# One-core cross-attention and ternary FFN: turning the second batch's operands by DMA, third scores moved forward, w2 loaded by GpSimd's queue

## The chip, the cores and the metric

One NeuronCore of a Trainium2 chip runs the whole kernel. The metric is the device time of one execution in microseconds (us). A core has TensorE (PE, matmul; PEld is its weight load), VectorE (DVE), ScalarE (ACT), GpSimd (POOL) and SyncE (SP), which here only issues DMAs. Each engine works through its own instructions in the order in which they are written, and stops where a semaphore has not reached the value waited for.

## The reference, cut to what matters

For each of B = 4 batches (512 rows of 512):

```
query, key = ctx @ Wq.T + bq, ctx @ Wk.T + bk     # ctx 512x256, Wq/Wk 128x256
probs      = softmax(query @ key.T)               # 512x512
x          = x + layernorm(x) @ probs
w1q, w2q   = ternary(w1), ternary(w2)             # clip(round(w / mean|w|), -1, 1)
h          = gelu(layernorm(x) @ w1q.T + b1)      # 2048 wide
out        = x + h @ w2q.T + b2
```

The scale of a ternary matrix is the mean over all of its 1M elements, so no weight can be rounded before the whole matrix has arrived and its absolute values are summed.

## The kernel before, in words

The program is written out engine by engine; nothing is scheduled automatically. `B1, W1, W2` number three sums over all partitions. Matmul operands of the attention and of the hidden layer are fp32 values split in two fp16 parts, "hi" (a cast on ACT) and "lo" (a subtraction on DVE), and must lie transposed in SBUF.

- `xn` (normalised x) and `probs` of a batch are written by POOL. For batches 0 and 1 (`b < EARLY`) PE transposes them in fp32 into PSUM (`turn_xn`, `turn_probs`, 16 transposes each, L454 and L467), ACT casts PSUM to the hi part (L661, L656) and DVE makes the lo part (L776, L770). For batches 2 and 3 ACT and DVE write hi and lo into a staging area in SBUF (L684, L689; L793, L799), and SP transposes each of the four by DMA (L258).
- `project` (L435) makes query and key, `scores` (L443) the score matrix, `attend` (L494) the attention: 12 matmuls for each of 4 row tiles. `maximum` (DVE, L804) and `exps` (ACT, L650) follow the scores; `residual` (DVE, L829) adds the attention to x; `moments2` (L835) and `aggregate2` make the statistics from which POOL (`layernorm2`, L373) writes `x2n`.
- `high_x2` (ACT, L674) and `low_x2` (DVE, L784) stage `x2n`, `turn_x2` and, for batch 0 in two halves, `turn_first_x2` (SP, L271) transpose it into `x2T`.
- `sum_abs` (ACT, L698) sums |w| of one of 8 chunks of a weight matrix, `abs_rows` (DVE, L849) adds the chunks, `total` (PE, L473) sums over partitions by a matmul with ones, `quantiser_scale` (DVE, L853) makes the scale. `round_weights` (POOL, L393 and L396) rounds chunk after chunk, `quantise` (DVE, L894) clips it, `turn_w1`, `turn_w2` (SP, L290, L298) transpose it.
- `hidden` (L511) is the first FFN matmul, in four groups of four 128-wide pieces; `first_output` (L525) and `output` (L536) are the second.

The place of the change is the stretch before the first `hidden`. On PE its order is written out by hand:

```
            scores(1, range(NT), lambda t: pe.wait_ge(xn0_read, t + 1))
            turn_xn(1)
            attend(0, lambda t: pe.wait_ge(exp_done, NT + t + 1), [0, 1])
            turn_probs(1)
            attend(0, lambda t: pe.wait_ge(exp_done, NT + t + 1), [2, 3])
            pe.wait_ge(bank_read[3], N_PROBS1 + 1)
            total(W1, ps_t[3])
```

then three tiles of `attend(1)`, `project(2)`, its fourth tile, `total(W2)`, `scores(2)`, and `hidden(0, 0)`. `hidden(0, 0)` waits for all four transposes of `x2T` of batch 0 and for the first piece of w1. The DMA queue of SP is likewise one list: loads of ctx, x, w1, w2, ctx again, b2 and x, and then the transposes.

Of the kernel before, what the change touches and what calls it, by code (L numbers as in the profile page):

```python
# [25 lines left out]
def xattn_ffn(nc, x, ctx_in, Wq, bq, Wk, bk, w1, b1, w2, b2, out):  # L26
# [4 lines left out]
    P = 128  # L31
# [10 lines left out]
    EARLY = 2  # L42
    LAST = B - 1
# [3 lines left out]
    with ExitStack() as stack:  # L47
# [109 lines left out]
        xnT_here = [sem(f"xnT_here{b}") for b in range(EARLY, B)]  # L157
        probsT_here = [sem(f"probsT_here{b}") for b in range(EARLY, B)]

# [82 lines left out]
        def _(sp):  # L242
# [9 lines left out]
            def load_w(m, h):  # L252
                n = raws[m].shape[1] // 4
                for i in (2 * h, 2 * h + 1):
                    sp.dma_start(raws[m][:, i * n:(i + 1) * n, :], w_views[m][:, i * n:(i + 1) * n, :]).then_inc(w_here[m][h], 16)
# [18 lines left out]
            def turn_xn(b):  # L274
                if b > EARLY:
                    sp.wait_ge(attn_ready, NT * b)
                sp.wait_ge(xn_hi_done, NT * (b - EARLY + 1))
                turn(xnT(b), xn_stage(b), 0, xnT_here[b - EARLY])
                sp.wait_ge(xn_lo_done, NT * (b - EARLY + 1))
                turn(xnT(b), xn_stage(b), 1, xnT_here[b - EARLY])  # L280

            def turn_probs(b):
                sp.wait_ge(probs_hi_done, NT * (b - EARLY + 1))
                turn(probsT(b), probs_stage(b), 0, probsT_here[b - EARLY])
                sp.wait_ge(probs_lo_done, NT * (b - EARLY + 1))
                turn(probsT(b), probs_stage(b), 1, probsT_here[b - EARLY])
# [38 lines left out]
            load_ctx(3)  # L325
            for c in range(NCH):
# [18 lines left out]
        def _(pool):  # L345
# [735 lines left out]
```

## Time and profile before

| | |
|---|---|
| median of 3 runs | 312.29 us (311.95 to 313.38) |
| profiled execution | 312.49 us, span of its trace 310.7 us |
| PE busy | 303.9 us, 98% of the span |
| DVE, ACT, POOL busy | 153.7, 143.9, 109.2 us |
| granted TensorE clock | 1.00 |
| first `hidden` matmul starts at | 59.32 us |

The profile counts from the start of the span. "Landing" of a DMA is the time from the start of its issue to its last completion. The chain of waits follows the work that ended last back to the beginning: each piece in it begins where the piece before it ended.

### The profile page before, as it was taken

How to read it: one execution, taken by the hardware profiler on the slowest of the kernel's cores; microseconds unless marked ns; L12 is line 12 of the kernel's file. 1: busy time of each engine (PE TensorE's matmuls, PEld its weight loads, DVE VectorE, ACT ScalarE, POOL GpSimd, SP SyncE). 2: the span in 40 equal slices, each digit the busy share in tenths (PEclk: the TensorE clock that was granted, in tenths of full speed). 3: DMA queues.
4: the chain of work that ended last, by engine and by line, in shares of the span. 5: the costliest groups of instructions: out<-in, count | busy, mean ns of one | idle time of the engine just before them, and what ended most of it. 6: DMA issues, size and time to landing. Idle time of an engine off the chain costs nothing.

```text
span 310.7 us, 3674 instructions
## 1 busy us (share of the span) xinstructions
PE 303.9 (98%) x1401; PEld 144.2 (46%) x1401; DVE 153.7 (49%) x295; ACT 143.9 (46%) x253; POOL 109.2 (35%) x111
## 2 busy tenths in 40 slices
PE   6799999999999999999999999999999999999996
PEld 3366544444444444444444444444444444444455
DVE  0888896764598853755308342445433003442101
ACT  2179998577723506542654604545440017762000
POOL 0276339999979960000903620000650000000000
PEclk9999999999999999999999999999999999999999
DMA  7899999674653992000032854000034100000011
GB/s 174 237 381 408 361 277 205 131 135 103 121 104 63 155 228 105 2 0 0 0 70 54 166 103 154 0 0 0 2 69 115 56 34 0 0 2 0 34 49 54
DMA packets 66706, 32.24 MB, mean 104 GB/s; under 512 B 59504, under 2 KB 60032, under 8 KB 66176
## 3 DMA queue, kind: packets, MB, share of 16 engines
q1 hardware_dynamic: 66368, 31.73, 40.4%
q10 hardware_dynamic: 320, 0.27, 0.4%
q8 instruction: 11, 0.18, 0.2%
q14 instruction: 7, 0.06, 0.1%
HBM read 15.21 MB, written 4.19 MB: 62 GB/s over the span
## 4 chain that ended last, share of the span: by engine, by line
PE 96%; DMA 2%; DVE 1%; SPq 0%; ACT 0%; issue 0%
PE ps_t L511 36%; PE ps_e L536 24%; PE ps_e L494 13%; PE ps_e L525 9%; PE ps_e L443 5%; PE ps_e L435 2%; PE ps_e L543 2%; PE ps_t L435 2%; DMA ctx_sb<-in_ctx 2%; PE ps_t L467 1%; PE ps_e L454 1%; PE ps_t L454 1%; SPq L247 0%; DVE ctxT L764 0%; ACT qkT L644 0%; DVE x_sb L1055 0%
## 5 line engine op out<-in xcount | busy, mean ns | idle before, releaser
L511 PE MATMUL ps_t<-x2T,w1T 128*128 128x512 f16 x512 | 112.1, 379 | 0.0
L706 ACT ACTIVATE ps_t<-ps_t,b_col 128x512 f32<-128x512 f32 x64 | 42.5, 665 | 96.6 <-PE ps_t L511 96.6
L511 PEld LDWEIGHTS ps_t<-x2T,w1T 128*128 128x128 f16 x512 | 50.1, 98 | 60.7 <-issue 0.6
L900 DVE SCALAR_TENSOR_TENSOR gT_lo<-ps_t,h_scale,gT_hi 128x512 f16<-128x512 f32 x64 | 45.1, 746 | 66.2 <-ACT gT_hi L711 66.2
L536 PE MATMUL ps_e<-w_raw,gT_hi 128*128 128x512 f16 x176 | 66.7, 379 | 0.0
L536 PE MATMUL ps_e<-w_raw,gT_lo 128*128 128x512 f16 x176 | 66.7, 379 | 0.0
L349 POOL TENSOR_TENSOR rstd<-var_eps,minus_half 128x4 f32<-128x4 f32 (+1 forms) x9 | 8.5, 947 | 99.7 <-DVE neg_mean L813 99.7
L711 ACT ACTIVATE gT_hi<-ps_t,h_scale 128x512 f16<-128x512 f32 x64 | 40.3, 684 | 0.0
L906 DVE SCALAR_TENSOR_TENSOR x_sb<-ps_e,h_unscale,x_sb 128x512 f32<-128x512 f32 x15 | 11.0, 748 | 57.9 <-PE ps_e L536 54.6
L536 PEld LDWEIGHTS ps_e<-w_raw,gT_lo 128*128 128x128 f16 x176 | 17.2, 98 | 21.4 <-issue 1.0
L536 PEld LDWEIGHTS ps_e<-w_raw,gT_hi 128*128 128x128 f16 x176 | 17.2, 98 | 21.1 <-issue 0.7
L525 PE MATMUL ps_e<-w_raw,gT_hi 128*128 128x512 f16 x64 | 24.3, 379 | 0.0
L525 PE MATMUL ps_e<-w_raw,gT_lo 128*128 128x512 f16 x64 | 24.3, 379 | 0.0
L494 PE MATMUL ps_e<-w_raw 128*128 128x512 f16 x96 | 21.7, 379 | 0.0
L387 POOL TENSOR_TENSOR x_sb<-x_sb,b_sb 128x512 f32<-128x512 f32 x16 | 21.0, 1343 | 0.0
L379 POOL TENSOR_SCALAR probs<-probs,row_inv 128x512 f32<-128x512 f32 x16 | 14.7, 935 | 17.3 <-DVE row_inv L809 17.3
L393 POOL TENSOR_SCALAR w_raw<-w_raw,inv_scale 128x1024 f32<-128x1024 f32 x16 | 20.8, 1301 | 0.0
L650 ACT ACTIVATE probs<-ps_e,row_max 128x512 f32<-128x512 f32 x16 | 10.9, 686 | 15.0 <-DVE row_max L804 14.7
L396 POOL TENSOR_SCALAR w_raw<-w_raw 128x1024 f16<-128x1024 f32 x16 | 17.2, 1074 | 1.4
L698 ACT ACTIVATE abs_out<-w_raw 128x1024 uint8<-128x1024 f32 x16 | 17.1, 1066 | 0.4
L443 PE MATMUL ps_e<-qkT 128*128 128x512 f32 x32 | 14.7, 598 | 0.7 <-ACT qkT L644 0.7
L494 PEld LDWEIGHTS ps_e<-w_raw 128*128 128x128 f16 x96 | 9.4, 98 | 11.3
(86 smaller groups left out, 290.9 us busy)
## 6 DMA issues: line engine op xcount, KB each, us to landing
w_raw<-in_L_ffn_w SPq DMA_DIRECT2D x8, 1024.0 KB, 14.7
x_sb<-in_x SPq DMA_DIRECT2D x4, 1024.0 KB, 7.5
out<-x_sb SPq DMA_DIRECT2D x15, 256.0 KB, 2.6
ctx_sb<-in_ctx SPq DMA_DIRECT2D x16, 128.0 KB, 3.2
b_sb<-in_L_ffn_b SPq DMA_DIRECT2D x1, 256.0 KB, 7.2
w_raw<-w_raw SPq DMA_TRANSPOSE x16, 3.8
out<-x_sb SPq DMA_DIRECT2D x2, 128.0 KB, 1.7
x2n<-in_L_xattn_Wq ACTq DMA_DIRECT2D x1, 128.0 KB, 3.0
```

The costliest lines, as they stand in the source:

```text
L387: nc.gpsimd.tensor_tensor(x_sb[:, b, t], x_sb[:, b, t], b2_sb[:], ALU.add).then_inc(b2_added, 1)
L393: nc.gpsimd.tensor_scalar(src, src, inv_scale[:, m:m + 1], ROUND, ALU.mult, ALU.add).then_inc(scaled, 1)
L396: nc.gpsimd.tensor_scalar(chunk_whole(m, c), src, -ROUND, 1.0, ALU.add, ALU.mult).then_inc(rounded, 1)
L443: nc.tensor.matmul(scores_bank(b, t)[:], qkT[:, 0, t * P:(t + 1) * P], qkT[:, 1], start=True, stop=True).then_inc(scores_ready, 1)
L494: mm = nc.tensor.matmul(attn_bank(b, t)[:], xnT(b)[:, u, j, t * P:(t + 1) * P], probsT(b)[:, v, j], start=(n == 0 and j == 0), stop=(n == ...
L511: mm = nc.tensor.matmul(ps_t[t][:], w1T[:, k, j], x2T[:, b % 2, v, :, j], start=(v == 0 and j == 0), stop=(v == 1 and j == ND - 1))
L525: mm = nc.tensor.matmul(y_bank(0, t)[:], part[:, k, t * P:(t + 1) * P], w2T[:, k], start=(k == 0 and part is gT_hi), stop=(k == NF - 1 and ...
L536: mm = nc.tensor.matmul(y_bank(b, t)[:], part[:, k, t * P:(t + 1) * P], w2T[:, k], start=(k == 0 and part is gT_hi), stop=(k == NF - 1 and ...
L698: nc.scalar.activation(abs_out[:], flat[:, c * CH:(c + 1) * CH], ACT.Abs, accum_out=abs_sum[:, m, c:c + 1]).then_inc(abs_done, 1)
L706: nc.scalar.activation(ps_t[t][:], ps_t[t][:], ACT.Gelu, scale=1.0 / LN_SCALE, bias=b1_col[:, k:k + 1]).then_inc(gelu_done, 1)
L711: nc.scalar.activation(gT_hi[:, k], ps_t[t][:], ACT.Identity, scale=h_scale[:, 0:1]).then_inc(gT_hi_done, 1)
L900: nc.vector.scalar_tensor_tensor(out=gT_lo[:, k], in0=ps_t[t][:], scalar=h_scale[:, 0:1], in1=gT_hi[:, k], op0=ALU.mult, op1=ALU.subtract) ...
```

## The change

Three things. First, batch 1 is handled as batches 2 and 3 are: ACT and DVE write hi and lo of `xn` and `probs` into staging areas (`x2T[:, 1]` and the upper half of `gT_lo`, not yet in use) and SP transposes them into `gT_hi` by DMA, so that PE no longer transposes them. Second, on PE `project(2)`, `total(W1)` and `scores(2)` stand between the whole of `attend(0)` and the whole of `attend(1)`, and `total(W2)` moves behind `hidden(0, 0)`. The lists of ACT and DVE are rewritten to match. Third, w2 is loaded by four DMAs of GpSimd's queue after `normalise_probs(1)`; on SP's queue the loads of b2 and of x of batches 2 and 3 go behind the transposes of w1.

```diff
+    BY_PE = 1
...
         def xn_stage(b):
+            if b < EARLY:
+                return x2T[:, 1].rearrange("p v h j t -> p v (h j t)")
             return w2_stage[:, 0]
...
         def probs_stage(b):
+            if b < EARLY:
+                return lo_stage[:, 1]
             return w2_stage[:, 1]
...
             load_x(1)
-            load_w(0, 0)
-            load_w(0, 1)
-            load_w(1, 0)
-            load_w(1, 1)
+            load_w1(0)
+            load_w1(1)
             load_ctx(2)
-            sp.dma_start(b2_sb[:], b2.rearrange("(a d) -> a d", a=1).to_broadcast([P, D])).then_inc(b2_here, 16)
-            load_x(2)
-            load_x(3)
+            turn_xn(1)
+            turn_probs(1)
             turn_first_x2(0)
             turn_w1(0)
             turn_first_x2(1)
...
             load_ctx(3)
+            sp.dma_start(b2_sb[:], b2.rearrange("(a d) -> a d", a=1).to_broadcast([P, D])).then_inc(b2_here, 16)
+            load_x(2)
+            load_x(3)
...
+            def load_w2():
+                for j in range(ND):
+                    pool.dma_start(w2_raw[:, j], w_views[1][:, j]).then_inc(w_here[1][j // 2], 16)
...
             normalise_probs(1)
+            load_w2()
             layernorm2(0, range(0, 2), 0)
...
-            turn_xn(1)
-            attend(0, lambda t: pe.wait_ge(exp_done, NT + t + 1), [0, 1])
-            turn_probs(1)
-            attend(0, lambda t: pe.wait_ge(exp_done, NT + t + 1), [2, 3])
-            pe.wait_ge(bank_read[3], N_PROBS1 + 1)
+            attend(0, lambda t: pe.wait_ge(exp_done, NT + t + 1), range(NT))
+            project(2, lambda s: pe.wait_ge(bank_read[s], N_PROBS0 + 1))
+            pe.wait_ge(bank_read[3], N_PROBS0 + 1)
             total(W1, ps_t[3])
-            attend(1, lambda t: pe.wait_ge(x2_done, t + 1), range(3))
-            project(2, lambda s: pe.wait_ge(bank_read[s], N_PROBS1 + 1))
-            attend(1, lambda t: pe.wait_ge(x2_done, t + 1), [3])
-            pe.wait_ge(total_read, W1 + 1)
-            total(W2, ps_t[3])
-            scores(2, range(NT), lambda t: pe.wait_ge(x2_done, NT + t + 1))
+            scores(2, range(NT), lambda t: pe.wait_ge(x2_done, t + 1))
+            attend(1, lambda t: pe.wait_ge(exp_done, NT * EARLY + t + 1), range(NT))
...
-            for g in range(GROUPS):
+            hidden(0, 0)
+            pe.wait_ge(x2_done, 2 * NT)
+            total(W2, ps_e[3])
+            for g in range(1, GROUPS):
                 hidden(0, g)
```

ScalarE's order at this place, from the exponentials of batch 1 on. In the rows L650 is `exps`, L661 and L656 the casts of the transposed `xn` and `probs`, L698 `sum_abs`, L674 `high_x2`, L644 the copy of query and key. Before:

```order
L650 ACTIVATE probs,row_sum<-ps_e,row_max 128x512 x4
L661 CAST gT_hi<-ps_t 128x512 x4
L698 ACTIVATE abs_out,abs_sum<-w_raw 128x1024 x4
L656 CAST gT_hi<-ps_t 128x512 x4
L698 ACTIVATE abs_out,abs_sum<-w_raw 128x1024 x2
L674 CAST gT_lo<-x2n 128x4x128 x2
L698 ACTIVATE abs_out,abs_sum<-w_raw 128x1024 x3
L674 CAST gT_lo<-x2n 128x4x128 x2
L698 ACTIVATE abs_out,abs_sum<-w_raw 128x1024 x4
L644 ACTIVATE qkT<-ps_t,bqk 128x512 x2
L698 ACTIVATE abs_out,abs_sum<-w_raw 128x1024
```

And of the change, where each line number is one lower and L683 and L688 write the staging areas:

```order
L649 ACTIVATE probs,row_sum<-ps_e,row_max 128x512 x4
L683 CAST x2T<-xn 128x4x128 x4
L688 CAST gT_lo<-probs 128x4x128 x4
L697 ACTIVATE abs_out,abs_sum<-w_raw 128x1024 x4
L643 ACTIVATE qkT<-ps_t,bqk 128x512 x2
L697 ACTIVATE abs_out,abs_sum<-w_raw 128x1024 x2
L673 CAST gT_lo<-x2n 128x4x128 x2
L649 ACTIVATE probs,row_sum<-ps_e,row_max 128x512 x4
L673 CAST gT_lo<-x2n 128x4x128 x2
L697 ACTIVATE abs_out,abs_sum<-w_raw 128x1024 x8
```

The copy of query and key of batch 2 now stands ahead of the last two absolute sums of w1; all eight of w2 stand behind the third exponentials.

VectorE's order around the first clipped weights. L784 is `low_x2`, L764 `turn_ctx(2)`, L829 `residual`, L894 `quantise`, L853 and L856 `quantiser_scale`. Before:

```order
L853 TENSOR_SCALAR scale<-ps_t 128x1
L856 RECIPROCAL inv_scale<-scale 128x1
L784 TENSOR_TENSOR gT_lo<-x2n,gT_lo 128x4x128 x2
L764 STREAM_TRANSPOSE ctxT<-ctx_sb 128x16x2x32
L829 SCALAR_TENSOR_TENSOR x_sb<-ps_e,x_sb 128x512
L784 TENSOR_TENSOR gT_lo<-x2n,gT_lo 128x4x128 x2
L894 TENSOR_SCALAR w_raw<-w_raw 128x1024
```

And of the change, where L846 is `abs_rows(W1)`, L801 `maximum` of batch 2, L806 `inverse`, and L781, L826 and L891 are `low_x2`, `residual` and `quantise`:

```order
L846 TENSOR_REDUCE abs_row<-abs_sum 128x1
L801 TENSOR_REDUCE row_max<-ps_e 128x1 x2
L850 TENSOR_SCALAR scale<-ps_t 128x1
L853 RECIPROCAL inv_scale<-scale 128x1
L801 TENSOR_REDUCE row_max<-ps_e 128x1 x2
L781 TENSOR_TENSOR gT_lo<-x2n,gT_lo 128x4x128 x4
L806 RECIPROCAL row_inv<-row_sum 128x1 x4
L826 SCALAR_TENSOR_TENSOR x_sb<-ps_e,x_sb 128x512
L891 TENSOR_SCALAR w_raw<-w_raw 128x1024
```

`low_x2` now stands behind the four maxima of batch 2, and the first `quantise` behind all of it.

## Rows read from the trace of the kernel before

**Rows 1.** The page: busy time of each engine.

```profile
PE 303.9 (98%) x1401; PEld 144.2 (46%) x1401; DVE 153.7 (49%) x295; ACT 143.9 (46%) x253; POOL 109.2 (35%) x111
```

**Rows 2.** Chain of waits in order of time: start, us, what.

```profile
27.79 1.75 PE ps_t L454 x16
29.54 5.18 PE ps_e L494 x24
...
41.85 7.79 PE ps_e L494 x36
49.64 3.43 PE ps_t L435 x8
...
55.78 3.54 PE ps_e L443 x8
59.32 27.63 PE ps_t L511 x128
```

**Rows 3.** Timeline of ScalarE: start, us, instruction, idle before and its releaser.

```profile
27.61 0.68 ACT L650 ACTIVATE probs<-ps_e,row_max 128x512 f32<-128x512 f32 x1
...
30.18 0.21 ACT L650 ACTIVATION_READ_ACCUMULATOR probs<-ps_e,row_max 128x1 f32 x1
...
43.25 1.06 ACT L698 ACTIVATE abs_out<-w_raw 128x1024 uint8<-128x1024 f32 x1
...
44.44 1.06 ACT L698 ACTIVATE abs_out<-w_raw 128x1024 uint8<-128x1024 f32 x1
...
174.69 2.16 ACT L689 CAST w_raw<-probs 128x512 f16<-128x512 f32 x4
```

**Rows 4.** Timeline of VectorE.

```profile
43.77 1.27 DVE L784 TENSOR_TENSOR gT_lo<-x2n,gT_lo 128x512 f16<-128x512 f32 x2
44.96 1.24 DVE L764 STREAM_TRANSPOSE ctxT<-ctx_sb 128x1024 f32<-128x1024 f32 x1
...
46.70 2.80 DVE L784 TENSOR_TENSOR gT_lo<-x2n,gT_lo 128x512 f16<-128x512 f32 x2
49.42 0.41 DVE L894 TENSOR_SCALAR w_raw<-w_raw 128x1024 f16<-128x1024 f16 x1
49.76 0.68 DVE L829 SCALAR_TENSOR_TENSOR x_sb<-ps_e,x_sb 128x512 f32<-128x512 f32 x1
...
58.70 1.36 DVE L804 TENSOR_REDUCE row_max<-ps_e 128x1 f32<-128x512 f32 x2
...
60.65 0.41 DVE L809 RECIPROCAL row_inv<-row_sum 128x1 f32<-128x1 f32 x4
```

**Rows 5.** Timeline of GpSimd.

```profile
28.93 2.69 POOL L379 TENSOR_SCALAR probs<-probs,row_inv 128x512 f32<-128x512 f32 x4 [2.55 <-DVE row_inv L809]
...
47.61 1.36 POOL L396 TENSOR_SCALAR w_raw<-w_raw 128x1024 f16<-128x1024 f32 x1
...
50.83 1.04 POOL L396 TENSOR_SCALAR w_raw<-w_raw 128x1024 f16<-128x1024 f32 x1
```

**Rows 6.** Timeline of SP's queue: issue start, us that issuing took.

```profile
49.87 1.45 SPq L290 DMA_TRANSPOSE w1T<-w_raw  x1
51.36 2.69 SPq L271 DMA_TRANSPOSE x2T<-gT_lo  x2
```

**Rows 7.** L271, the transpose issued at 52.7 alone.

```profile
DMA to landing us min/median/max: 3.3/3.3/3.3
```

**Rows 8.** L255, the fourth load of w1 alone, issued at 13.55.

```profile
DMA to landing us min/median/max: 15.5/15.5/15.5
```

**Rows 9.** L255, all loads of w1 and w2; the last has the longest landing.

```profile
L255 SPq DMA_DIRECT2D w_raw<-in_L_ffn_w x8: 507/694/3829, 11.7 to 21.8; - x8
...
DMA to landing us min/median/max: 9.3/14.7/17.8
```

**Rows 10.** L258, transposes of a whole staged half (16 blocks), all eight.

```profile
DMA to landing us min/median/max: 4.3/4.7/5.0
```

**Rows 11.** Timeline of TensorE, its first matmuls.

```profile
1.17 4.21 PE L428 MATMUL ps_e<-gT_lo 128*128 128x512 f16 x10 [1.17 <-DVE gT_lo L910]
```

More of the change, by code:

```diff
@@ L156, in xattn_ffn @@
         x2T_here = [sem(f"x2T_here{b}") for b in range(B)]
-        xnT_here = [sem(f"xnT_here{b}") for b in range(EARLY, B)]
-        probsT_here = [sem(f"probsT_here{b}") for b in range(EARLY, B)]
+        xnT_here = [sem(f"xnT_here{b}") for b in range(BY_PE, B)]
+        probsT_here = [sem(f"probsT_here{b}") for b in range(BY_PE, B)]
         ident_zero, ident_done = sem("ident_zero"), sem("ident_done")
@@ L250, in load_x, with load_w1 @@
                 sp.dma_start(x_sb[:, b], x_tiles[b]).then_inc(x_here[b], 16)
[L252 to L253 removed]
+            def load_w1(h):
+                n = NF // 4
                 for i in (2 * h, 2 * h + 1):
[L255 removed]
+                    sp.dma_start(w1_raw[:, i * n:(i + 1) * n], w_views[0][:, i * n:(i + 1) * n]).then_inc(w_here[0][h], 16)
             def turn(dst, stage, v, here):
@@ L276, in turn_xn @@
                     sp.wait_ge(attn_ready, NT * b)
[L277 to L280, printed above, removed]
+                sp.wait_ge(xn_hi_done, NT * (b - BY_PE + 1))
+                turn(xnT(b), xn_stage(b), 0, xnT_here[b - BY_PE])
+                sp.wait_ge(xn_lo_done, NT * (b - BY_PE + 1))
+                turn(xnT(b), xn_stage(b), 1, xnT_here[b - BY_PE])
             def turn_probs(b):
[L283 to L286, printed above, removed]
+                sp.wait_ge(probs_hi_done, NT * (b - BY_PE + 1))
+                turn(probsT(b), probs_stage(b), 0, probsT_here[b - BY_PE])
+                sp.wait_ge(probs_lo_done, NT * (b - BY_PE + 1))
+                turn(probsT(b), probs_stage(b), 1, probsT_here[b - BY_PE])
             def turn_w1(c):
@@ L479, in attend @@
                         for j in range(NT):
-                            if t == 0 and b < EARLY:
+                            if t == 0 and b < BY_PE:
                                 if n == 0 and j == 0:
@@ L660, in high_turned_xn @@
                     act.wait_ge(xnT_ready, ND * b + j + 1)
-                    nc.scalar.copy(xnT(b)[:, 0, j], xn_bank(b, j)[:]).then_inc(xnT_hi_done, 1)
+                    nc.scalar.copy(xnT(b)[:, 0, j], ps_e[j][:]).then_inc(xnT_hi_done, 1)
             def high_x2(b, tiles=range(NT)):
@@ L726, in _ @@
             exps(1)
-            high_turned_xn(1)
-            sum_abs(0, (2, 3, 4, 5))
-            high_turned_probs(1)
+            high_xn(1)
+            high_probs(1)
+            sum_abs(0, range(2, 6))
+            copy_qk(2)
             sum_abs(0, (6, 7))
             high_x2(0, (0, 1))
-            sum_abs(1, (0, 1, 2))
+            exps(2)
             high_x2(0, (2, 3))
-            sum_abs(1, range(3, 7))
-            copy_qk(2)
-            sum_abs(1, (7,))
-            exps(2)
+            sum_abs(1, range(NCH))
             act.wait_ge(h_scale_done, 1)
@@ L939, in _ @@
             aggregate2(0, (0, 1))
-            low_turned_probs(1)
+            low_probs(1)
             residual(0, 2)
             moments2(0, 2)
-            abs_rows(W1)
             residual(0, 3)
@@ L946, in _ @@
             aggregate2(0, (2, 3))
+            abs_rows(W1)
+            maximum(2, 0)
+            maximum(2, 1)
             quantiser_scale(W1, ps_t[3])
+            maximum(2, 2)
+            maximum(2, 3)
             low_x2(0, (0, 1))
-            turn_ctx(2)
+            low_x2(0, (2, 3))
+            for t in range(NT):
+                inverse(2, t)
             residual(1, 0)
-            low_x2(0, (2, 3))
             quantise(0, 0)
@@ L956, in _ @@
             quantise(0, 2)
-            abs_rows(W2)
             residual(1, 3)
             quantise(0, 3)
-            maximum(2, 0)
-            maximum(2, 1)
-            quantiser_scale(W2, ps_t[3])
-            maximum(2, 2)
-            maximum(2, 3)
             quantise(0, 4)
-            for t in range(NT):
-                inverse(2, t)
+            abs_rows(W2)
             quantise(0, 5)
@@ L974, in _ @@
             low_gelus(0, (2, 3))
+            quantiser_scale(W2, ps_e[3])
             low_gelus(0, (4, 5))
```

62 lines of the change are left out of this document (28 added, 34 removed).

## The prediction

> **What bounds the kernel now.** I read the page first, for whether one engine is busy throughout: TensorE (PE) is, 98% of the span [rows 1]. Busy shares say nothing of single stages, so I read the chain of waits next, for the stretch that the change touches. From the end of the scores of batch 1 at 27.79 to the first `hidden` matmul at 59.32 every piece is PE work that begins where the one before ended [rows 2]; behind 59.32 the same holds to the last output. So the question is one date: when does `hidden(0, 0)` start after the change? Each us by which it moves moves the end, unless something later becomes bound. The timelines of ACT, DVE, POOL and SP are read for durations, to date what PE will wait for.
>
> **What PE is relieved of.** Two blocks of 16 transposes, 1.75 us each: 3.5 us [rows 2]. Attention tiles keep their price, 5.18 for two, so 10.4 for a batch; `project` is 3.4 and `scores` 3.5 [rows 2]. If nothing waited, `hidden(0, 0)` would start at 59.3 - 3.5 = 55.8.
>
> **New wait 1: attention without cover.** In the trace the transposes of batch 1's `xn` fill PE until 29.54. Now `attend(0)` stands right behind the scores and its first tile writes the bank that `exps(1)` reads. That exponential ends at 27.61 + 0.68 = 28.3 [rows 3], so PE idles 0.5. `attend(0)` ends at 28.3 + 10.4 = 38.7. `project(2)` needs ctx of batch 2: it now follows w1 alone in SP's queue. The fourth load of w1 landed at 13.55 + 15.5 = 29.0 [rows 8]; the four of w2, now gone from this place, landed by 21.8 + 17.8 = 39.6 [rows 9], so each MB takes 2.65 us. Half a MB of ctx lands 1.3 us behind w1 if it moves as fast, up to twice or more in its shorter pieces; I take 31.5. DVE turns it in 1.2 [rows 4], long before 38.7. `project(2)` ends at 42.1.
>
> **New wait 2: the sum over w1.** `total(W1)` stands behind `project(2)` and ahead of `scores(2)`. Its input comes from ACT, through eight sums. ACT ends `exps(1)` at 30.4 [rows 3]. Then come 8 casts in SBUF at 0.54 (2.16 for four, [rows 3]): 34.7; `probs` are ready by 28.93 + 2.69 = 31.6 [rows 5]. Four sums at 1.19 (from start to start, 43.25 to 44.44, [rows 3]): 39.4. Then the copy of batch 2's query and key, whose second half waits for PE at 42.1; an ACT pass of this size takes 0.68 [rows 3]: 42.8. Only then the last two sums: 45.2. DVE may be as late. From 31.5 it has ctx 1.2, four residuals and four statistics passes at about 0.7 each (the residual's 0.68, [rows 4]; estimate for the other), 5.6, eight subtractions, and about 1 of small ones. Two subtractions took 1.27 in one place and 2.80 in another [rows 4]; POOL writes `x2n` during two of the eight, so 6 x 0.64 + 2 x 1.4 = 6.6, in all 14.4: 45.9, less some 0.5 that such instructions overlap at their ends. I take 45.4 for both, `total(W1)` at 45.6: PE idles 3.5 us. `scores(2)` to 49.1, `attend(1)` to 59.5 (`exps(2)` is ready: first scores at about 46.5, maximum 0.7, exponential 0.7, 47.9). The two waits, 0.5 and 3.5, have eaten the 3.5 that the transposes gave, to within the 0.2 by which 59.5 differs from 59.3.
>
> **What queues behind `total(W1)`, and new wait 3.** DVE cannot take the maxima of batch 2 until `scores(2)` is out, and `low_x2` stands behind all four. The last maximum is ready at 49.1 + 0.7 = 49.8 (1.36 for two, [rows 4]). Four subtractions of `low_x2` follow, while POOL rounds w1 (its rounding starts when `quantiser_scale(W1)` is through, behind the second maximum, at about 48.2). The row for this pair is in the trace: two subtractions took 2.80, from 46.70 to the next instruction at 49.42, or 1.36 each, and POOL's rounding beside them 1.36 where it took 1.04 alone [rows 4, 5]. The other end is the quiet row, 1.27 for two, 0.64 each. I take 1.36, because that row is the same instruction against the same rounding: 49.8 + 5.4 = 55.2. Then four reciprocals 0.4, `residual(1, 0)` 0.7, `quantise(0, 0)` 0.4 [rows 4]: 56.7. SP issues `turn_w1(0)` only now, 1.3 (1.45 in its row, 1.35 for each of the two behind it, [rows 6]): 58.0. Behind it in SP's queue stand the two transposes of the second half of x2: the hi part issues in 1.3, to 59.3, and the lo part lands 3.3 after its issue starts [rows 7]: 62.6. `hidden(0, 0)` needs all of them and starts at 62.7 instead of 59.3: **+3.4 us**. In the trace the same four stand with room: the lo part, issued at 52.7, landed at 56.0, 3.3 before PE came.
>
> The Trainium skill (GPSIMD Engine Reference, section Key points) says that GpSimd shares its SBUF interfaces with VectorE and that they contend where a Vector instruction has two SBUF inputs. By that rule `low_x2`, which has two, runs slow against the rounding and the sum is the one above; by the quiet row alone it would be 2.9 us less. The rows at 46.70 agree with the rule.
>
> **The w2 load.** POOL is free from 31.6 to about 38.7, when `layernorm2(0)` may begin; no row shows a DMA issued by POOL. Nothing at the low end; at the high end the four could cost the whole 7 us without delaying anybody, and a further 4, since ACT comes for `x2n` at 45.2. So nothing. It arrives about 32 + 10.6 = 43, ACT wants it at about 52. `sum_abs(1)` ends at 52 + 8 x 1.19 = 61.5, before gelu's first input at 62.7 + 1.7. `round_weights(1)` waits for the total of w2, now behind `hidden(0, 0)`: it starts some 2.5 us later with respect to `hidden` than before. The turned w2 is wanted first when all of `hidden(0)` is through, 27.6 us behind its start [rows 2], so I cost that at nothing, and the later loads of b2 and of x of batches 2 and 3 too, which are used only after the rounding. If this cover were gone, PE would stall at the first matmuls of `first_output`.
>
> But w2 moves at the same time as the transposes of batch 1's `xn` and `probs`, which used to have no counterpart. The last of the four can issue at 42.6 and lands 4.7 later [rows 10], 47.3, before 49.1. That is one bound: no cost. If the transposes got no DMA time before w2 ended at 43 to 44.5, the four would follow at about 2.6 each (twice the 1.35 of a half-size one, [rows 6]): 54.9, and `attend(1)` would end at 65.3. I take the first, since neither bound adds to wait 3 until `attend(1)` starts 3 us late.
>
> The Trainium skill (DMA: Bandwidth & Descriptors, section SWDGE vs HWDGE vs iDMA) says that GpSimd's and SP's DMAs feed different queues between which each DMA engine goes round, packet by packet. By it neither starves. Nothing in the trace before shows it.
>
> **Sum.** 312.49 (the profiled execution) + 3.4 = 315.9. The median of the runs is 0.2 lower, so 315.7.
>
> **Rivals.** About 0.5% (1.6 us) is what a measurement of this kernel can tell from no change.
>
> (1) *VectorE wins against POOL*, the case on the other side: not slower. `hidden(0, 0)` starts at 57.3 + 4d, where d is one subtraction of `low_x2`. At d = 0.64 it is 59.9, +0.6: 312.9. It decides at d = 0.9: below that the change is inside 0.5%. For it: the quiet row. Against it: the row at 46.70. Also here: ACT or DVE a little quicker at 45.4. Chance 0.23.
>
> (2) *The transposes pay in full*: PE gives back 3.5 and the sum over w1 is there in time, 309.0. ACT would have to be through at 42.1, but two sums stand behind a copy that itself waits for 42.1. The rows exclude most of it; what remains is a downstream gain that I don't see. Chance 0.04.
>
> (3) *w2 starves the transposes*: `hidden(0, 0)` at 65.3, +6.0: 318.3. For it: loads back to back take 2.65 per MB and leave no room. Against it: nothing says that SP's transposes come last; with equal shares they are only a few us later, and have 1.8 to spare. Chance 0.14.
>
> (4) *TensorE's clock falls in the new idle stretches.* The granted clock is given as 1.00 for the whole trace (table above), yet the first ten matmuls took 4.21 us [rows 11], 0.42 each, where the same shape later takes 0.216 (5.18 for 24, [rows 2]): the lower of the levels 1.2 and 2.4 GHz, after nothing had run. If 3.5 us without work bring that back, 2.1 us are lost each time, as over those ten: 317.8, or 319.9 for both stretches. No idle stretch of this length lies between matmuls of the trace. The Trainium skill (TensorE: Matmul & The Clock Gate, section Why this matters for your kernels) warns that gaps without work between bursts of matmuls bring the lower clock back; no run here shows it yet. Chance 0.09.
>
> The forecast itself, +1.7 to +5 from wait 3, keeps 0.50. **Numbers:** slower 0.50 + 0.14 + 0.09 = 0.73, same 0.23, faster 0.04. Range 312.6 to 318.6: the low end takes in the lower ends of wait 3, the high end starvation and one clock fall; outside are about one in ten on each side.
>
> **What would show it.** In the changed kernel's chain: PE idle about 0.5 before `attend(0)`, waiting for `exps`; about 3.5 before `total(W1)`, waiting for `abs_rows`; about 3 before `hidden(0, 0)`, waiting for a DMA of `x2T`. `low_x2` at 1.36 each beside `round_weights(0)`. `hidden` starts at 62.7. The prediction is wrong if `attend(1)` waits for `probsT`, if `hidden(0, 0)` starts with no DMA wait, if matmuls at 0.42 stand behind a stall, or if PE stalls again behind `hidden`.

## The result and the profile after

The changed kernel takes 319.35 us in the median (317.36 to 320.02, 4 runs) against 312.84 us (311.95 to 313.77, 4 runs) of the kernel before: a ratio of 1.0205 with a 95% interval of 1.0171 to 1.0239. It is slower, as forecast, but by more than the 315.7 us and outside the range that ended at 318.6. Ratios, here and below, leave out a run more than 1.5% above the fastest of its kernel (323.41 in experiment 4, 318.36 in experiment 7), while medians and ranges hold every run.

The profiled execution took 317.36 us with a span of 315.6 us. Its granted clock is 0.994 in the mean; in the other three runs it is 0.989. The page, busy times and the transfers that GpSimd's queue made:

```profile
PE 302.6 (96%) x1369; PEld 141.0 (45%) x1369; DVE 156.9 (50%) x295; ACT 144.2 (46%) x253; POOL 112.1 (36%) x115
...
q0 software_dynamic: 576, 4.19, 3.5%
```

PE was busy for 98% of a shorter span [rows 1], with 6.8 us idle (310.7 - 303.9); now 13.0 us are idle (315.6 - 302.6). The chain of waits from the end of `project(2)` to the landing that the first `hidden` waits for shows where (the counterpart of [rows 2]):

```profile
41.98 0.02 issue
42.01 0.69 ACT qkT L643
42.70 1.04 ACT abs_out L697 x2
43.74 0.02 issue
43.76 1.16 ACT abs_out L697 x2
44.92 0.02 issue
44.94 0.17 DVE abs_row L846
45.12 0.14 issue
45.25 0.36 PE ps_t L475 x2
45.61 5.24 PE ps_e L450 x8
50.85 0.02 issue
50.88 0.69 DVE row_max L801
51.57 4.92 DVE gT_lo L781 x4
56.48 0.25 DVE row_inv L806 x4
56.74 0.59 DVE x_sb L826
57.33 0.44 DVE w_raw L891
57.77 0.02 issue
57.78 1.23 SPq L292
59.02 0.04 issue
59.06 1.33 SPq L273
60.40 0.04 issue
60.44 3.39 DMA x2T<-gT_lo
```

Where the chain was PE alone, it now leaves PE twice: for the last absolute sums of w1 (42.0 to 45.2), and from the last score on for maximum, `low_x2`, residual, clipping, two SP issues and a landing (50.9 to 63.8). That is the order of steps in the forecast. `hidden(0, 0)` starts at 63.87, 1.2 later than forecast and 4.55 later than before; from there to the end of the span it is 251.7 us, against 251.4 before (310.7 - 59.32), so no later stall was added. PE started that `hidden` 0.04 us behind the last landing, but it had hardly waited for it: `attend(1)` ended at 63.75 (53.23 + 10.52). Of the four signs of being wrong that the prediction names, two are plainly there, `attend(1)` waiting for transposes and `hidden(0, 0)` starting without a DMA wait worth the name, and the third, matmuls at the lower clock behind a stall, follows below.

TensorE's timeline for the same place shows two things that the forecast did not have, a wait before `attend(1)` for transposes and long scores:

```profile
28.00 10.53 PE L494 MATMUL ps_e<-w1T 128*128 128x512 f16 x48 [1.63 <-ACT probs L649]
...
45.25 0.36 PE L475 MATMUL ps_t<-abs_row,ones 128*128 128x1 f32 x2 [3.28 <-DVE abs_row L846]
45.47 5.37 PE L450 MATMUL ps_e<-qkT 128*128 128x512 f32 x8
53.23 10.52 PE L494 MATMUL ps_e<-gT_hi 128*128 128x512 f16 x48 [2.39 <-DMA gT_hi<-gT_lo]
```

The second batch's scores, the same eight matmuls, took 3.54 before [rows 2]. A row of the table of stretches (start and end, length, PE busy, granted clock, DMA share, GB/s) gives the reason: behind 3.28 us without work the clock was at the lower of its levels for part of the stretch. 0.29 of 5.8 us is 1.7 us lost, and 5.24 - 3.54 is 1.7.

```profile
45.20:51.00 5.80, 5.59 (x10) 0.71 1.20 244
```

And the transposes. SP issued the first of the four at 32.05, and issuing it alone took 10.03 us and landing 14.2. It is the hi part of `xn`, of the form whose landing was 4.3 to 5.0 before [rows 10]. The four loads of w2 from GpSimd's queue kept their pace. First the row of that transpose with its landing, then that of the loads:

```profile
L260 SPq DMA_TRANSPOSE gT_hi<-x2T x1: 10030/10030/10030, 32.0 to 32.0; - x1
...
DMA to landing us min/median/max: 14.2/14.2/14.2
```

```profile
L403 POOL DMA_DIRECT2D w_raw<-in_L_ffn_w x4: 537/546/771, 31.1 to 33.0; - x4
...
DMA to landing us min/median/max: 5.6/8.5/11.7
```

The loads landed between 31.1 + 5.6 = 36.7 and 33.0 + 11.7 = 44.7, 2.67 us for each MB; on SP's queue it was 2.65. The transpose landed at 46.3, behind all of w2. This is close to the starved bound of the forecast (nothing moves before w2 ends at 43 to 44.5), not to the free one.

The other three landed in 6.0, 4.6 and 5.2 us, the last of them at 53.1, and `attend(1)` started at 53.2, where the starved bound had 54.9.

So after the trace there were two theories. **A**: waits 1 to 3 as forecast, and on top a fall of TensorE's clock behind the new idle stretches, once in the profiled execution and, if their mean clock is read so, twice in the runs at 0.989. **B**: w2 on GpSimd's queue starves SP's transposes, and late `attend(1)` is what costs.

### The profile page after: what moved, and what is told of

It is laid out like the page before. It is cut to its first block, busy times and chain, and to the rows that moved or that the text cites. A ratio compares the mean times of both kernels' runs of the same rounds, so it can differ in the third digit from the quotient of the medians.

```text
span 315.6 us, 3613 instructions
## 1 busy us (share of the span) xinstructions
PE 302.6 (96%) x1369; PEld 141.0 (45%) x1369; DVE 156.9 (50%) x295; ACT 144.2 (46%) x253; POOL 112.1 (36%) x115
## 3 DMA queue, kind: packets, MB, share of 16 engines
q0 software_dynamic: 576, 4.19, 3.5%
HBM read 15.21 MB, written 4.19 MB: 62 GB/s over the span
## 4 chain that ended last, share of the span: by engine, by line
PE 85%; DVE 6%; DMA 4%; ACT 2%; SPq 2%; issue 0%; DVEq 0%
PE ps_t L511 35%; PE ps_e L538 24%; PE ps_e L494 10%; PE ps_e L527 9%; PE ps_e L450 3%; DMA ctx_sb<-in_ctx 3%; PE ps_e L545 2%; DVE gT_lo L781 2%; ACT probs L649 1%; PE ps_t L442 1%; PE ps_e L442 1%; DMA x2T<-gT_lo 1%; SPq L249 1%; DVE ctxT L761 1%; DVE w1T L767 1%; DVE w1T L773 1%
## 5 line engine op out<-in xcount | busy, mean ns | idle before, releaser
L395 POOL TENSOR_SCALAR w_raw<-w_raw,inv_scale 128x1024 f32<-128x1024 f32 x16 | 20.0, 1250 | 8.8 <-DVE inv_scale L853 8.8
L450 PE MATMUL ps_e<-qkT 128*128 128x512 f32 x32 | 16.4, 655 | 0.9 <-ACT qkT L643 0.9
L362 POOL TENSOR_SCALAR xn<-x_sb,neg_mean,rstd 128x512 f32<-128x512 f32 x16 | 14.4, 913 | 0.4
```

The costliest lines, as they stand in the source:

```text
L395: nc.gpsimd.tensor_scalar(src, src, inv_scale[:, m:m + 1], ROUND, ALU.mult, ALU.add).then_inc(scaled, 1)
L450: nc.tensor.matmul(scores_bank(b, t)[:], qkT[:, 0, t * P:(t + 1) * P], qkT[:, 1], start=True, stop=True).then_inc(scores_ready, 1)
```

## The experiments

Every time below is a median, with its ratio to runs of the kernel before on the same chip. Lines are those of each kernel.

**1. Matmuls that fill the two waits.** To the changed kernel, 14 matmuls into an unused bank ahead of `total(W1)` and 18 ahead of `attend(1)`.

```diff
             project(2, lambda s: pe.wait_ge(bank_read[s], N_PROBS0 + 1))
             pe.wait_ge(bank_read[3], N_PROBS0 + 1)
+            fill(14, 0)
             total(W1, ps_t[3])
             scores(2, range(NT), lambda t: pe.wait_ge(x2_done, t + 1))
+            fill(18, 0)
             attend(1, lambda t: pe.wait_ge(exp_done, NT * EARLY + t + 1), range(NT))
```

> The change, with matmuls that compute nothing needed (into a free PSUM bank) in TensorE's two new idle stretches: 14 ahead of total(W1), 18 ahead of attend(1). Theory A (two falls of the granted clock, 1.8 us each, make the median 2 us longer than the profiled run, which had one): the granted clock is 1.00 throughout, scores(2) takes 3.45 and not 5.24, attend(1) still starts at about 53.2 when the transposed probs land, hidden(0,0) at 63.5; profiled time about 317.0, median of the runs 317 instead of 319.35, and a spread of the runs under 0.5 us. Rival (the spread of the runs has another cause, such as the DMAs): the median stays at 319 and the spread at 2.5 us.

317.37 us (316.54 to 318.02, 4 runs), 1.0151 [1.0112, 1.0190]; the clock was 0.999 or 1.00 in all four.

```profile
45.45 3.68 PE L454 MATMUL ps_e<-qkT 128*128 128x512 f32 x8
...
53.60 10.52 PE L498 MATMUL ps_e<-gT_hi 128*128 128x512 f16 x48 [0.59 <-DMA gT_hi<-gT_lo]
64.30 7.08 PE L515 MATMUL ps_t<-x2T,w1T 128*128 128x512 f16 x32 [0.17 <-DMA x2T<-gT_lo]
```

The scores are short again and the ratio is 0.5% lower, 1.7 us, which is only just clear of the noise. The gain is over the runs at 0.989. Over the profiled execution of the changed kernel, which had a single fall and took 317.36, there is none (317.79 here), because `attend(1)` still starts at 53.6 and `hidden(0, 0)` no earlier: the starved transposes hold it as soon as the clock does not.

**2 to 4. Half of w2 later; x2 first; both.** In experiment 2 the second half of w2 is issued behind `layernorm2(0, (2, 3))`. In experiment 3 the first two `low_x2` stand ahead of the maxima and both halves of x2 ahead of w1. Experiment 4 has both edits.

```diff
-            load_w2()
+            load_w2((0, 1))
...
             layernorm2(0, range(2, NT), 1)
+            load_w2((2, 3))
```

```diff
             turn_first_x2(0)
-            turn_w1(0)
             turn_first_x2(1)
+            turn_w1(0)
...
             abs_rows(W1)
+            low_x2(0, (0, 1))
             maximum(2, 0)
...
-            low_x2(0, (0, 1))
             low_x2(0, (2, 3))
```

> The change, with the second half of w2 loaded only after layernorm2(0, 2..3). Theory B (the w2 load and the four new transposes share the DMA engines and each waits for the other; freed of it attend(1) starts when scores(2) is out, but low_x2 and turn_w1(0) hold hidden(0,0) at 63.8 as well): the four transposes land by 50.5, attend(1) starts near 51, hidden(0,0) still at 63.5 to 63.9, the time as for the change. Rival (starvation of the transposes alone set the date): hidden(0,0) starts at 61.3, 2.5 us earlier.

317.94 us (316.87 to 318.84, 4 runs), 1.0170 [1.0128, 1.0211].

> The change, with low_x2 of the first two tiles ahead of the maxima of batch 2 on VectorE, and the second half of x2 ahead of the first piece of w1 on SP. Theory B: x2T lands at about 60, but attend(1) still starts at 53.2, when the transposed probs land, so hidden(0,0) starts at 63.5, 0.3 earlier; no change of the time. Rival (the forecast's: low_x2 and turn_w1(0) alone hold hidden(0,0)): hidden(0,0) starts at 61.3 or before, 2.5 us earlier.

318.04 us (316.92 to 319.21, 4 runs), 1.0180 [1.0128, 1.0232].

> The edits of the two kernels before together. Theory B (two chains of nearly equal length): only now hidden(0,0) starts earlier, at 61.3, with attend(1) from 51; 2.5 us off the change, about 314.9 profiled. Rival (one of the chains alone set the date): nothing more than what that kernel alone gave.

318.41 us (315.69 to 323.41, 4 runs), 1.0157 [1.0091, 1.0222]. The row of `hidden(0, 0)` in experiment 2, those of the scores and of `hidden(0, 0)` in 3, and those of `attend(1)`, `hidden(0, 0)` and the last of the four transposes in 4:

```profile
64.10 7.08 PE L512 MATMUL ps_t<-x2T,w1T 128*128 128x512 f16 x32 [1.43 <-DMA x2T<-gT_lo]
```

```profile
46.15 6.41 PE L450 MATMUL ps_e<-qkT 128*128 128x512 f32 x8
...
64.08 7.07 PE L511 MATMUL ps_t<-x2T,w1T 128*128 128x512 f16 x32
```

```profile
53.82 12.21 PE L495 MATMUL ps_e<-gT_hi 128*128 128x512 f16 x48 [3.44 <-DMA gT_hi<-gT_lo]
65.86 5.34 PE L512 MATMUL ps_t<-x2T,w1T 128*128 128x512 f16 x24
```

```profile
L260 SPq DMA_TRANSPOSE gT_hi<-gT_lo x1: 3572/3572/3572, 43.7 to 43.7; - x1
...
DMA to landing us min/median/max: 10.0/10.0/10.0
```

None of the three can be told from the changed kernel by its time. Removing one chain leaves the other: in 2 `hidden` waits for x2 (wait 3), in 3 it follows `attend(1)` without a wait. The two together should have removed both, and did not, because the late half of w2 held up the last transpose as the early half had done: issued at 43.7, it landed 10.0 us later at 53.7, behind a load of w2 that GpSimd issued at 45.2 and that landed at 53.5. Experiment 4 also shows a second fall: behind 3.44 us without work, `attend(1)` took 12.21 us instead of 10.52, and the mean clock of that execution is 0.989. But experiment 3 read 0.989 with one long fall, its scores taking 6.41 behind a wait of 3.28. So a mean of 0.989 says that about twice as much was lost as at 0.995, not that the clock fell twice.

**5. w2 on SP's queue,** half ahead of the four transposes, half behind them: theory B by itself.

```diff
             load_ctx(2)
+            load_w2((0, 1))
             turn_xn(1)
             turn_probs(1)
+            load_w2((2, 3))
             turn_first_x2(0)
```

> The change, with w2 loaded again by SP's queue, in which nothing overtakes: half of it ahead of the four transposes of batch 1, half behind them. Theory B2 (DMAs of GpSimd's queue keep SP's transposes waiting; attend(1) starts when the last one has landed; low_x2 and turn_w1(0) are the second chain): the last transpose lands by 47.5, TensorE does not wait for it, attend(1) starts at 49.1 or, with one fall of the clock, 50.9; hidden(0,0) starts at 62 to 63.8, held by x2T, for which TensorE now waits 2 to 3 us. The forecast's wait 3 alone. Rival (the DMA engines are simply full, whoever issues): the last transpose lands at 52 or later as before, attend(1) at 53.

316.88 us (316.64 to 317.01, 4 runs), 1.0160 [1.0133, 1.0186]; clock 0.994 or 0.995 in all.

```profile
45.49 5.38 PE L451 MATMUL ps_e<-qkT 128*128 128x512 f32 x8
50.70 10.52 PE L495 MATMUL ps_e<-gT_hi 128*128 128x512 f16 x48
63.07 7.08 PE L512 MATMUL ps_t<-x2T,w1T 128*128 128x512 f16 x32 [1.85 <-DMA x2T<-gT_lo]
```

```profile
DMA to landing us min/median/max: 4.6/4.6/4.6
```

That is the last of the four transposes, issued at 40.9 and landed at 45.5, and `attend(1)` has no wait. The edit changes both the queue and the dates of w2. What tells them apart is the last transpose of experiment 4: in both kernels half of w2 was issued behind it (1.5 us behind it there, 2.6 here, at 43.5), and it landed in 10.0 us with the loads on GpSimd's queue, in 4.6 with them on its own. So the queue counts, and not the bytes alone. `hidden(0, 0)` moves only from 63.87 to 63.07, because wait 3 stands behind it. All four runs read 0.994 or 0.995, where three of four of the changed kernel read 0.989: with the wait before `attend(1)` the larger loss of clock is gone.

**6. The forecast's case alone:** experiment 5 with fillers, 14 ahead of `total(W1)` and 8 ahead of `hidden(0, 0)`, so that neither starvation nor the clock counts.

```diff
+            fill(14, 0)
             total(W1, ps_t[3])
...
+            fill(8, 1)
             hidden(0, 0)
```

> f1_w2_sp_split (the change with w2 on SP's queue) with matmuls that compute nothing needed in the two idle stretches that it has left: 14 ahead of total(W1), 8 ahead of hidden(0,0). Theory A and B2: with neither late transposes nor a fall of the clock, only what the prediction's sum priced is left, the wait for the sum over w1 and wait 3: scores(2) takes 3.5, attend(1) starts at 49.1, hidden(0,0) at 61.3 to 62.7, clock 1.00 in every run, 314.5 to 315.9 us, 1.8 less than f1 at most. Rival (the clock is not what scores(2) lost its 1.8 us to): scores(2) still takes 5.2 and the time stays at 316.9.

316.01 us (315.09 to 317.22, 4 runs), 1.0136 [1.0105, 1.0166], clock 1.00 in all. TensorE, then VectorE:

```profile
45.89 3.68 PE L455 MATMUL ps_e<-qkT 128*128 128x512 f32 x8
49.41 10.52 PE L499 MATMUL ps_e<-gT_hi 128*128 128x512 f16 x48
...
62.62 7.08 PE L516 MATMUL ps_t<-x2T,w1T 128*128 128x512 f16 x32 [0.96 <-DMA x2T<-gT_lo]
```

```profile
50.22 5.00 DVE L788 TENSOR_TENSOR gT_lo<-x2n,gT_lo 128x512 f16<-128x512 f32 x4
```

`hidden(0, 0)` at 62.62, where the forecast had 62.7.

**7 and 8. The chain shortened.** Experiment 7 is 5 with the edits of 3. Experiment 8 puts `scores(2)` ahead of `total(W1)`, two maxima ahead of `abs_rows(W1)`, and both halves of x2 ahead of w1.

```diff
+            scores(2, range(NT), lambda t: pe.wait_ge(x2_done, t + 1))
             total(W1, ps_t[3])
-            scores(2, range(NT), lambda t: pe.wait_ge(x2_done, t + 1))
...
-            abs_rows(W1)
             maximum(2, 0)
             maximum(2, 1)
-            quantiser_scale(W1, ps_t[3])
+            abs_rows(W1)
             maximum(2, 2)
             maximum(2, 3)
+            quantiser_scale(W1, ps_t[3])
```

> The same with low_x2 of two tiles ahead of the maxima and the second half of x2 ahead of the first piece of w1. Theory B2: both chains are now short; attend(1) from 49.1 (50.9 with a clock fall), hidden(0,0) right behind it at 59.5 to 61.3: 313 to 315 us. Rival (there is a third limit at 63): hidden(0,0) stays at 63.

314.87 us (313.16 to 318.36, 9 runs), 1.0081 [1.0050, 1.0111].

> w2 on SP's queue as in the two before, the second half of x2 ahead of w1, and scores(2) ahead of total(W1), the maxima and abs_rows in that order too. Theory C (the 3.3 us wait for the sum over w1 is what ate the saving of the transposes, and the same wait makes the clock fall): TensorE works on scores(2) while ACT sums, idles under 1 us, the granted clock is 1.00 in every run, attend(1) from about 47, hidden(0,0) at 57.5 to 60.5, held by the DMA engines; 310.5 to 313.5 us, as fast as the kernel before or a little faster. Rival (the four transposes keep the attention late anyway): attend(1) at 50 or later and no gain over the kernel with w2 on SP and x2 first.

314.44 us (313.49 to 317.73, 4 runs), 1.0101 [1.0038, 1.0164]. `hidden(0, 0)` in 8:

```profile
59.99 8.75 PE L512 MATMUL ps_t<-x2T,w1T 128*128 128x512 f16 x32 [2.19 <-issue]
```

In 7 `hidden(0, 0)`, at 62.35, follows `attend(1)` without a wait: wait 3 is gone and 2.0 us of the median with it, though the wait for the sum was 4.16 in its profiled execution. The scores of that execution took 6.02 behind it, one long fall at a mean clock of 0.988. In 8 the scores no longer wait for the sum, and `hidden(0, 0)` starts at 59.99, 0.7 behind the kernel before. It had waited 2.19, by the dates for the first piece of w1 at the end (issued at 56.4, landed 3.5 later; the last transpose of `x2T` had landed at 58.45), and the clock fell behind that wait. Its two runs at a clock of 1.00 took 313.74 and 313.49, still 1.5 to 1.8 above the 311.95 of the kernel before; the others, at 0.995 and 0.988, 315.15 and 317.73.

**9 and 10. One part of the change on the kernel before.** Experiment 9 is the kernel before with w2 on GpSimd's queue. Experiment 10 adds the new order on PE, but lets PE go on transposing batch 1. Around it its lists differ from those of the change, in three places that bear on the stretch: ACT copies query and key of batch 2 behind all sums of w1, DVE makes two `low_x2` ahead of the maxima, and SP takes both halves of x2 ahead of w1.

```diff
-            load_w(1, 0)
-            load_w(1, 1)
...
             normalise_probs(1)
+            load_w2()
```

```diff
+            project(2, lambda s: pe.wait_ge(bank_read[s], N_PROBS1 + 1))
             pe.wait_ge(bank_read[3], N_PROBS1 + 1)
             total(W1, ps_t[3])
-            attend(1, lambda t: pe.wait_ge(x2_done, t + 1), range(3))
-            project(2, lambda s: pe.wait_ge(bank_read[s], N_PROBS1 + 1))
-            attend(1, lambda t: pe.wait_ge(x2_done, t + 1), [3])
-            pe.wait_ge(total_read, W1 + 1)
-            total(W2, ps_t[3])
-            scores(2, range(NT), lambda t: pe.wait_ge(x2_done, NT + t + 1))
+            scores(2, range(NT), lambda t: pe.wait_ge(x2_done, t + 1))
+            attend(1, lambda t: pe.wait_ge(exp_done, NT * EARLY + t + 1), range(NT))
```

> The kernel before with one part of the change alone: w2 loaded by GpSimd's queue after normalise_probs(1), everything else as it was. Theory B2: here no transpose of DMA stands on the way until 42, and w2 is through by 44; x2T of the first half lands up to 3 us later than 52.0, still ahead of hidden(0,0) at 59.3: no change, within 0.5%. Rival (the part costs by itself, for instance through a late absolute sum of w2 on ACT): 1 us or more.

311.94 us (311.36 to 313.38, 10 runs), 0.9998 [0.9973, 1.0022].

> e6_w2_gpsimd_only (the kernel before with w2 on GpSimd's queue) with the second part of the change alone: project(2), total(W1), scores(2) between attend(0) and attend(1), total(W2) behind hidden(0,0), batch 1 still turned by TensorE, the second half of x2 ahead of w1. Theory C (the move costs nothing where the sum over w1 is ready when TensorE comes, and the 32 transposes on TensorE give ACT that time): TensorE waits nowhere over 0.3 us, clock 1.00, hidden(0,0) at 59.3 to 60, 312 to 313 us. Rival (the move is what costs, by the maxima and low_x2 behind it): hidden(0,0) at 61 or later, 314 us.

312.97 us (312.01 to 313.80, 6 runs), 1.0033 [1.0013, 1.0052]. Its scores:

```profile
45.52 3.70 PE L446 MATMUL ps_e<-qkT 128*128 128x512 f32 x8 [1.01 <-ACT qkT L649]
```

The queue of w2 costs nothing while there is no transpose for it to overtake. The new order, in this version, costs about 1 us while PE's transposes cover it: they bring `project(2)` at 40.80 where the changed kernel has it at 38.37, `total(W1)` follows it at 44.23 without a wait, and in place of the 3.28 there is one wait of 1.01, for the copy of query and key. The transposes by DMA alone, with the old order, were not run. What is shown is that the third part costs nothing by itself and the second, with it, need not cost more than 1 us as long as PE keeps its transposes; the rest of the loss comes with taking them away.

**11 and 12. Half of the cover kept.** Experiment 11 is 8 with `xn` of batch 1 transposed by PE again, and `probs` by DMA. Experiment 12 adds another order behind `hidden(0, 0)`: ACT's first gelus ahead of the eighth sum of w2, `total(W2)` behind `hidden(0, 1)`, `low_gelus` ahead of the late clips.

```diff
             scores(1, range(NT), lambda t: pe.wait_ge(xn0_read, t + 1))
+            turn_xn(1)
             attend(0, lambda t: pe.wait_ge(exp_done, NT + t + 1), range(NT))
```

```diff
             hidden(0, 0)
+            hidden(0, 1)
             pe.wait_ge(x2_done, 2 * NT)
             total(W2, ps_e[3])
...
-            sum_abs(1, range(NCH))
+            sum_abs(1, range(7))
             act.wait_ge(h_scale_done, 1)
+            gelus(0, 0)
+            sum_abs(1, (7,))
```

> f3_w2_sp_scores_first with xn of batch 1 turned by TensorE again and only probs by DMA. Theory D (the DMA engines are full between 31 and 60 and set hidden(0,0) in f3; two transposes fewer free 5.2 us there, while TensorE's 1.75 us fall into the time in which it waits for exps(1) anyway): attend(1) from 46.8, hidden(0,0) at 57.2 to 58.5 instead of 60.0, clock 1.00, 310 to 311.5 us, faster than the kernel before. Rival (ACT and DVE, not the DMA engines, set it): hidden(0,0) stays at 59.5 to 60, 313 us.

315.50 us (313.89 to 317.10, 4 runs), 1.0116 [1.0066, 1.0166].

```profile
57.07 7.07 PE L521 MATMUL ps_t<-x2T,w1T 128*128 128x512 f16 x32
...
67.38 4.87 PE L521 MATMUL ps_t<-x2T,w1T 128*128 128x512 f16 x14 [3.13 <-DVE gT_lo L908]
```

`hidden(0, 0)` comes at 57.07, ahead of every other kernel here, and PE gives it back 7 us later: it waits 3.13 for DVE's `low_gelus`. DVE stood at the clipping of a chunk that POOL had not rounded, and ACT had come to the first gelu only at 59.04, behind its sums. Part of the lead was also luck: the scores of batch 1 began at 22.75 there and at 24.19 in the profiled execution of before (22.97 in experiment 9, whose `hidden(0, 0)` began at 58.10), so the kernel itself gained about 0.8 us (34.3 from those scores to `hidden(0, 0)`, 35.1 in experiment 9), not the 2.3 that I used next.

> The kernel with xn of batch 1 turned by PE and probs by DMA (scores before the sum, second half of x2 before w1), and behind hidden(0, 0) another order: ACT takes the first gelus ahead of the eighth absolute sum of w2, PE takes total(W2) behind hidden(0, 1), DVE takes the first low_gelus ahead of the clipping of chunks 5 to 7. In the earlier version hidden(0, 0) came at 57.07, 2.3 us ahead of the kernel before, and then PE stalled 3.13 us for low_gelus. Theory A (the gain was lost in that stall and in the clock fall that it brought): no stall above 0.5 us before the second block of hidden, granted clock 1.00 or close to it, 310.0 to 311.0, ratio 0.993 to 0.996 to the kernel before. Rival B (the stretch is bound by POOL's rounding or by w2 arriving as late as before, the gain moves to a stall at first_output): PE waits 2 us or more at the first matmuls of first_output or in hidden(0, 2) for a piece of w1, and 312 to 314. Rival C (the short waits before scores(2) and total(W1) by themselves bring a clock fall): no stall behind hidden but a stretch of some 3.4 us at a granted clock near 0.5, 312.0 to 312.8.

317.30 us (315.81 to 317.56, 6 runs), 1.0161 [1.0139, 1.0183]. The stall is gone. Rival B of that expectation is the nearest: the gain went to a stall at `first_output`, of 1.47 where it said 2 or more, but the time lies above its 312 to 314, and the clock of 0.995 in five runs comes on top. POOL's timeline at the start of w2's rounding, then PE:

```profile
75.66 1.12 POOL L401 TENSOR_SCALAR w_raw<-w_raw,inv_scale 128x1024 f32<-128x1024 f32 x1 [6.28 <-DVE inv_scale L867]
```

```profile
87.98 0.39 PE L537 MATMUL ps_e<-w_raw,gT_hi 128*128 128x512 f16 x1 [1.47 <-DMA w_raw<-w_raw]
...
124.64 2.53 PE L504 MATMUL ps_e<-w_raw 128*128 128x512 f16 x11 [1.96 <-DMA w_raw<-w_raw]
```

POOL sat idle 6.28 us. Three of the edits meet there: ACT's eighth sum ended at 68.6, `total(W2)` stood at 72.39 behind the second block of `hidden`, and DVE took `low_gelus` of four more pieces ahead of the scale, which it made at 75.22. Which of the three weighs most was not run. Rounding late, POOL fed the first transpose of w2 late, at 78.5, and that one took 9.5 us to land (3.0 to 3.3 in the kernel before); two 1 MB loads of x had gone into the same queue at 75.4 and 75.9, the second of which landed at 85.4. The debt came back twice: as 1.47 at the first matmuls of `first_output`, and as 1.96 before the attention of batch 2, whose operands POOL makes after the rounding. The profiled execution, at a clock of 1.00, is the fastest with 315.81; the other five, at 0.995, took 317.09 to 317.56. No kernel of the twelve beats the kernel before.

## Why the prediction was wrong, step by step

The step that failed is the one from the three waits to the sum. The sum put two things at nothing: what TensorE's clock loses behind the idle stretch of the forecast's own wait 2, and what w2 takes from the transposes beside it. The runs showed both, and they cost most together. A smaller error is the size of wait 1.

**PE's relief and wait 1.** The relief of 3.5 and the date of `attend(0)` were right (28.00 for 28.3). The wait was 1.63, not 0.5: PE's front end was 1.4 earlier in this execution (`scores(1)` at 22.77, in the trace of before at 24.19), but the exponentials only 0.4 (27.17 for 27.61). The forecast subtracted its terms from a single execution whose PE was late at the start. In the kernel before an early start is kept (from `scores(1)` to `hidden(0, 0)` it is 35.1 us both there and in experiment 9, which started it at 22.97); after the change it is lost at this wait, which was between 0.64 and 1.73 in the profiled executions of experiments 1 to 8.

**Wait 2 was right.** `total(W1)` at 45.25 for 45.6, an idle stretch of 3.28 for 3.5, released by ACT's last sums as written.

**Wait 3 was right.** Experiment 6 is the forecast's case with neither of the two terms that were put at nothing: `low_x2` in 5.00 us for 5.4, `hidden(0, 0)` at 62.62 for 62.7. Its 316.01 us are 4.2 above the kernel before on that chip (311.79), for 3.4 forecast; the missing 0.8 is about what wait 1 was short of (1.73 for 0.5). In the changed kernel itself the chain of wait 3 held too, 12.3 us from the last maximum to the landing for 12.8, but PE came as late by another way and did not wait there. One subtraction took 1.25 in the mean, beyond the 0.9 from which the rival decides by which VectorE wins.

**The clock is the term that was left out.** I listed it as a rival with a chance of 0.09 and put nothing of it in the sum, although the forecast itself has PE idle for 3.5 us and the first matmuls of the trace [rows 11] show the lower level. Measured: 1.7 us for a fall (5.24 against 3.54), one in the profiled run; by their mean clock of 0.989 the other three lost about twice as much, in two falls as in experiment 4 or in one long one as in experiments 3 and 7 (2.9 and 2.5 us on the scores), which cannot be told without a profile. Filling the waits took 0.5% off the ratio (experiment 1). The same 3.28 without work brought the fall in experiments 2 to 5 as well, and the 4.16, 3.44 and 3.13 of experiments 7, 4 and 11 did too, while waits up to 2.02 (experiment 2, before its first `project`) did not in any profiled execution; in between it varied (2.39 did not in the changed kernel, 2.19 did in experiment 8). It is not the same in each execution: two of nine runs of experiment 7 kept 1.00. The warning of the Trainium skill (TensorE: Matmul & The Clock Gate, section Why this matters for your kernels) holds here, and should have been a term. My price, 2.1, was near for a single fall; the chance was wrong.

**"I take the first": the transposes beside w2.** The forecast chose the bound at which they cost nothing. They were starved: 14.2 us for a landing of 4.3 to 5.0 [rows 10], `attend(1)` at 53.2 instead of 49.1. In the profiled execution that moved `hidden(0, 0)` by nothing, since the clock fall and wait 3 led to the same date beside it; it decides when the clock is kept (64.30 in experiment 1 against 62.62 in 6), and it makes a second idle stretch, behind which the clock fell again in experiment 4. That this happened in the three runs at 0.989 of the changed kernel is argued from their mean clock. The sentence from the Trainium skill (DMA: Bandwidth & Descriptors, section SWDGE vs HWDGE vs iDMA) was read wrongly. It speaks of turns by packet, and "neither starves" does not follow from it: the page of the profile gives 576 packets for 4.19 MB on GpSimd's queue, 7.3 KB each, and between 28 and 50 us of that trace SP's queue moved 1.70 MB in 6747 packets, 0.25 KB each. Equal turns would leave the transposes a small part of the bytes. That this is the mechanism is argued; that the loads on GpSimd's queue are the cause is shown by experiments 4 and 5.

**The sum of it.** By ratios, waits 1 to 3 are 1.4% (experiment 6), and clock and starvation together another 0.7% (1.0205 - 1.0136), some 2 us. These two do not add up one by one, because they meet in the same stretch: starvation alone is 1.0151 (experiment 1), the clock alone 1.0160 (experiment 5), and neither stands clear of 1.0136, but both together are 1.0205. The median of the changed kernel holds the larger loss of clock, which its profiled execution (317.36, inside the range) does not. The forecast had the two as rivals that exclude each other, with 0.14 and 0.09; its range is said to take in starvation and one clock fall, but by its own figures the two together come to 318.3 + 2.1 = 320.4, and the range ended at 318.6. The cover behind `hidden` held as forecast; experiment 12 shows stalls of 1.47 and 1.96 when w2 is rounded later still.

What stays open: how long PE may idle before the clock falls, and why executions of one kernel differ in it. Even the kernel before, whose trace has no wait over 1.2 us, read 0.995 in three of its 43 runs beside the experiments, the ones of 314.18, 314.19 and 314.62 us.

## What to carry to other kernels

Work on the bounding engine that looks like a cost may be what covers a chain of small steps on the others; before taking it away, date the chain (sums, a scale, maxima, a landing) and see whether it fits in what is left. If the sum of a forecast has the matmul engine idle for some 3 us, as here, the clock's price belongs in the sum, and two rivals that can both happen need a sum in which they do. Bulk loads moved to another queue are not free for what runs beside them: ask which small-packet transfers share the time, and what waits for them.

## What the runs showed of the hardware

A DMA transpose that shares its time with 1 MB loads of GpSimd's queue took 10.03 us to issue and 14.2 to land, while the loads lost nothing (2.67 us per MB). With w2 on SP's own queue, half of it ahead of the four transposes and half behind, the first landed in 6.1 and the last in 4.6 (experiment 5); with the second half behind them on GpSimd's queue the last took 10.0 (experiment 4). Plain loads ahead in its own queue delay a transpose as well: 9.5 us to land behind two 1 MB loads of x (experiment 12), where the eight of its kind took 3.0 to 3.3 in the kernel before.

Issuing a 1 MB load cost GpSimd 0.54 to 0.77 us (the row of the loads above), 2.4 us for four, with nobody waiting.

POOL loses time beside VectorE too. While `low_x2` ran at 1.25 us for each subtraction, where the quiet row has 0.64 [rows 4], a rounding step that takes 1.12 us elsewhere in the same trace (at 58.63) took 2.06, and one of 1.04 [rows 5] took 1.36:

```profile
52.44 2.06 POOL L395 TENSOR_SCALAR w_raw<-w_raw,inv_scale 128x1024 f32<-128x1024 f32 x1
54.59 1.36 POOL L398 TENSOR_SCALAR w_raw<-w_raw 128x1024 f16<-128x1024 f32 x1
```
